# Adjacency masks cast to bf16 by GpSimd's transfers, and new hand-written orders, in a four-layer graph network

## What is computed

```
x = _layernorm(x + _L0_gnn_ref(x, adj, W0, a_src, a_dst))   # graph attention
x = _layernorm(x + _L1_gnn_ref(x, adj, W1, a1))             # graph attention
x = _layernorm(x + _L2_gnn_ref(x, adj, a0..a3, bias2))      # sigmoid attention
x = _layernorm(x + _L3_gnn_ref(x, adj, W3, bias3))          # relational conv
# layers 0 and 1: h = x @ W.T; e_ij = leaky_relu(h_i.a_src + h_j.a_dst, 0.2)
#   e = where(adj == 0, -inf, e); alpha = softmax(e, -1); return alpha @ h
# layer 2: e = leaky((x * a0) @ x.T, 0.2); alpha = sigmoid(where(adj == 1, e, -max))
#   return alpha @ x + bias2
# layer 3: h = (adj == 1) @ x; return h @ W3[0] + bias3
```

## Time and profile before

| | us |
|---|---|
| median of 3 runs | 260.65 (260.47 to 260.87) |
| the profiled execution | 259.62 |
| its span, first to last instruction | 257.1 |
| TensorE busy | 228.6 |
| VectorE busy | 226.5 |
| ScalarE busy | 206.5 |
| GpSimd busy | 173.6 |

### The profile page before, as it was taken

The page is one execution under the profiler, slowest core; times in us unless marked ns, Lnnn a source line. Parts: engine busy times, 40 slices in busy tenths (PEclk is TensorE's granted clock), DMA queues, the critical chain, the costliest instruction groups (busy, mean ns, idle before and its releaser), DMA issues.

```text
span 257.1 us, 5794 instructions
## 1 busy us (share of the span) xinstructions
PE 228.6 (89%) x1745; PEld 207.1 (81%) x1745; DVE 226.5 (88%) x794; ACT 206.5 (80%) x634; POOL 173.6 (67%) x248
## 2 busy tenths in 40 slices
PE   6869898998988999999999999999999988989670
PEld 6769788986977999879898888898979877887560
DVE  0498999989998999989999999999989998998851
ACT  3797999986867999878359965986895959989874
POOL 1003031759789988697357999867596876799892
PEclk9999999999999999999999999999999997999995
...
GB/s 243 402 387 213 209 92 259 166 18 0 1 85 0 126 124 134 71 41 46 41 125 82 3 1 0 42 4 51 34 0 3 3 42 42 42 41 0 43 41 129
DMA packets 12145, 21.77 MB, mean 85 GB/s; under 512 B 1104, under 2 KB 5968, under 8 KB 12112
## 3 DMA queue, kind: packets, MB, share of 16 engines
...
...
## 4 chain that ended last, share of the span: by engine, by line
PE 35%; DVE 23%; ACT 19%; POOL 13%; issue 6%; DMA 1%; POOLq 0%; DVEq 0%; ACTq 0%
PE banks L1176 13%; PE banks L1116 6%; POOL frstd L541 6%; DVE wgt_all L857 5%; DVE fstats L907 5%; PE banks L1143 4%; ACT odd_square L601 4%; POOL fxTa L565 4%; ACT xs_all L678 3%; PE banks L1173 3%; PE banks L1153 3%; DVE fres_all L899 3%; ACT wgt_all L651 3%; PE banks L1133 2%; ACT vals_all L636 2%
## 5 line engine op out<-in xcount | busy, mean ns | idle before, releaser
L541 POOL TENSOR_TENSOR frstd<-fvar,minus_half 128x4 f32<-128x4 f32 x64 | 65.1, 1020 | 36.5 <-ACT fvar L684 29.3
L1176 PE MATMUL banks<-vals_all,wgt_all 128*128 128x129 f32 x512 | 64.0, 279 | 3.4 <-issue 2.5
L1176 PEld LDWEIGHTS banks<-vals_all,wgt_all 128*128 128x128 f32 x512 | 60.6, 194 | 5.1 <-issue 3.1
L857 DVE SCALAR_TENSOR_TENSOR wgt_all<-banks,gain,mask_all 128x256 f32<-128x256 f32 x128 | 52.7, 471 | 1.9 <-PE banks L1133 1.9
L536 POOL TENSOR_TENSOR xb_all<-xs_all,bias_cen 128x256 f32<-128x256 f32 x64 | 45.5, 736 | 8.7 <-ACT xs_all L678 4.0
L907 DVE BATCH_NORM_STATS2 fstats<-fres_all 128x6 f32<-128x256 f32 x128 | 47.8, 417 | 0.5
L678 ACT ACTIVATE xs_all<-fres_all,frstd 128x128 f32<-128x128 f32 x124 | 39.5, 399 | 6.1 <-POOL frstd L541 6.0
L1143 PE MATMUL banks<-fxT,fxTa 128*128 128x256 f32 x128 | 31.3, 386 | 1.8 <-DVE wgt_all L865 0.6
L1176 PE MATMUL banks<-xs_all,wgt_all 128*128 128x128 f32 x256 | 31.4, 276 | 0.4 <-DVE wgt_all L865 0.4
L1176 PEld LDWEIGHTS banks<-xs_all,wgt_all 128*128 128x128 f32 x256 | 29.9, 192 | 0.9 <-DVE wgt_all L865 0.4
L565 POOL TENSOR_SCALAR fxTa<-fxT,w_pack 128x256 f32<-128x256 f32 x28 | 25.6, 930 | 6.4 <-ACT fxT L616 6.4
...
## 6 DMA issues: line engine op xcount, KB each, us to landing
...
```

The source lines that it names most:

```text
L541: nc.gpsimd.tensor_tensor(frstd[:, int(l), slot(n), :], fvar[:, int(l), slot(n), :], minus_half[:, :, :], ALU.pow).then_inc(fast_pool[k], 1)
L857: last = nc.vector.scalar_tensor_tensor(out=wgt(u)[:, c, :], in0=place(f"rows{l}", u), scalar=gain[:, u, c, 1:2], in1=maskT(u)[:, c, :], o ...
L1176: last = nc.tensor.matmul(place(f"out{l}", u)[:, b * width:(b + 1) * width], wgt(u)[:, c, b * P:(b + 1) * P], (vals if l in "01" else xs)( ...
```

## The change

The masks come from GpSimd's own transfers, which read int32 and write bf16 (`cast_mask`). The ring is as deep as there are teams, so all sixteen are issued first thing and never wait for a buffer; each has a semaphore of its own. The ring `adj_all` and SyncE's sixteen loads are gone, and so are ScalarE's mask steps; `seen` reads the mask. The masks are now 0 and 1, so `res2` multiplies by 0.5 instead, in the same instruction as its addition, and `w3_cen` isn't doubled. `xTa` of all teams and `norm1` of all teams are ScalarE's (before: 2 and 7 of the 16). VectorE has `norm2` of 2 teams instead of 1, `low` of 2 instead of 1, and `bias2` of one. All lists and the table of banks are written anew: before, teams 0 to 5 went through layers 0 and 1 together, and the last four ended in the order 13, 14, 15, 12; now the teams follow each other in a stagger, and after the start with teams 0 to 2 a new one comes in about as often as one leaves.

```diff
-X_IN, XT_IN, ADJ, MASK, XS, FXT, FXTA, VALS, WGT, SG, FRES, XB = 4, 3, 4, 10, 6, 7, 5, 6, 7, 2, 9, 5
-EDGE = 0.5
+X_IN, XT_IN, MASK, XS, FXT, FXTA, VALS, WGT, SG, FRES, XB = 4, 3, 16, 6, 7, 5, 6, 7, 2, 9, 5
 ORDER = {
     "sp": (
-        "xT:0 adj:0 adj:1 xT:1 xT:2 adj:2 adj:3 x:0 x:2 x:1 x:3 weights:0 xT:3 weights:2 weights:1 adj:4 xT:4 xT:5 "
+        "xT:0 x:0 xT:1 x:1 xT:2 weights:1 x:3 x:2 weights:0 weights:2 xT:3 xT:4 xT:5 x:4 x:5 x:6 xT:6 xT:7 x:7 xT:8 x:8 "
...
     "pool": (
-        "pow0:0 pow0:1 var0:2 pow0:2 var0:3 pow0:3 var0:4 pow0:4 pow1:0 norm1:0 bias2:0 pow0:5 xTa:0 pow1:1 bias2:1 "
+        "mask:0 mask:1 mask:3 mask:2 mask:4 mask:5 mask:10 mask:8 mask:6 mask:7 mask:9 mask:11 mask:12 mask:14 mask:15 "
+        "mask:13 var0:0 pow0:0 pow0:1 pow0:2 pow1:0 bias2:0 pow1:1 var0:3 pow0:3 pow1:2 bias2:1 bias2:2 var0:4 pow0:4 "
...
         @block.gpsimd
+            def cast_mask(l, n, k):
+                nc.gpsimd.dma_start(mask_all[:, pair(n, MASK), :, :], adj_turned[n]).then_inc(fast_mask_in[n], 16)
...
             def note_odd(l, n, k):
-                act.wait_ge(fast_adj_in[n % ADJ], loaded(n * H, ADJ))
+                act.wait_ge(fast_mask_in[n], 16)
...
-                nc.scalar.activation(odd_square[:, :, :, :], adj_all[:, pair(n, ADJ), :, :], ACT.Square, bias=minus_half[:, 0, 0:1],
+                nc.scalar.activation(odd_square[:, :, :, :], mask_all[:, pair(n, MASK), :, :], ACT.Square, bias=minus_half[:, 0, 0:1],
                                      accum_out=odd[:, n:n + 1]).then_inc(fast_act[k], 1)
-            def make_mask(l, n, k):
-                if n >= MASK:
-                    act.wait_ge(fast_pe[(n - MASK) % K], at("pe", "agg", final(n - MASK)))
-                act.wait_ge(fast_adj_in[n % ADJ], loaded(n * H, ADJ))
-                for u in graphs(n):
-                    nc.scalar.activation(maskT(u)[:, :, :], adj_in(u)[:, :, :], ACT.Copy, scale=EDGE).then_inc(fast_act[k], 1)
...
-                nc.vector.tensor_scalar(w3_cen[:, :], w3_cen[:, :], 1 / EDGE, None, ALU.mult).then_inc(w3_cen_set, 1)
...
             def weights(l, n, k):
                 dve.wait_ge(fast_pe[k], at("pe", f"rows{l}", final(n)))
                 if l == "0":
-                    masker = doer("mask", n)
-                    dve.wait_ge(signals[masker][k], at(masker, "mask", final(n)))
+                    dve.wait_ge(fast_mask_in[n], 16)
...
-                    nc.vector.tensor_tensor(fres_all[:, pair(n, FRES), :, :], gathered, xb_all[:, pair(n, XB), :, :], ALU.add).then_inc(fast_dve[k], 1)
+                    nc.vector.scalar_tensor_tensor(out=fres_all[:, pair(n, FRES), :, :], in0=gathered, scalar={"2": 0.5, "3": 1.0}[l],
+                                                   in1=xb_all[:, pair(n, XB), :, :], op0=ALU.mult, op1=ALU.add).then_inc(fast_dve[k], 1)
```

More of the change, by code:

```diff
@@ L418, in res_gnn_kernel @@
         biases_in = sem("biases_in")
[L419 removed]
+        fast_mask_in = [sem(f"fast_mask_in_{q}") for q in range(TEAMS)]
         fast_xT_in = [sem(f"fast_xT_in_{q}") for q in range(XT_IN)]
@@ L576, in scales @@
                 nc.gpsimd.tensor_tensor(fscale[:, slot(n), :], vals_all[:, pair(n, VALS), :, D], frstd[:, 0, slot(n), :], ALU.mult).then_inc(fast_pool[k], 1)
-            steps = {"bias": biases, "pow": powers, "low": low_part, "var": variances, "fscale": scales, "xTa": scale_xTa, "norm": normalize}
+            steps = {"mask": cast_mask, "bias": biases, "pow": powers, "low": low_part, "var": variances, "fscale": scales, "xTa": scale_xTa, "norm": normalize}
             for step, l, n in order("pool"):
@@ L939, in judge @@
                 nc.vector.tensor_reduce(bad[:, 8:9], bad[:, 3:7], AX.X, ALU.max).then_inc(bad_step, 1)
-            steps = {"mask": make_mask, "high": high_part, "umax": larger, "bias": biases, "low": low_part, "norm": normalize, "fscale": scales, "logits": logits, "peak": peak, "dmax": largest,
+            steps = {"high": high_part, "umax": larger, "bias": biases, "low": low_part, "norm": normalize, "fscale": scales, "logits": logits, "peak": peak, "dmax": largest,
                      "weight": weights, "rsum": row_sums, "rinv": inverses, "alpha": alpha, "res": residual,
```

31 lines of the change are left out of this document (8 added, 23 removed), and 192 rows, old and new, of tables (BANKS, ORDER).

## The result

The changed kernel takes 258.63 us, median of 20 runs (257.13 to 260.89); the kernel before took 260.60 in the same series (259.45 to 261.65). The ratio is 0.9922, 95% interval 0.9902 to 0.9943. The forecast was 259.1. So the time is right within half a microsecond, and the kernel is faster by 0.8%. Of the four terms behind the forecast none came out with its size, and they don't add up to the measured gain; the last part says how the number came out right all the same. A ratio here leaves out executions more than 1.5% above the fastest of the same kernel, while a median is of all, so a ratio needn't be the quotient of the two medians.

What follows compares the result with a forecast made beforehand. TensorE (228.6 us of 257.1) and VectorE (226.5) were taken to bind, with fill and tail. Terms +5.4 - 3.1 + 1.0 - 4.8 = -1.5 on 259.62 gave 258.1; with 1.03 to the median, 259.1; range 252.0 to 265.5.

Steps and rivals of the forecast that it cites:

- Term 1: Where the last layer 1 product ends: work moved ahead of that point puts it 5.4 us later, at 225.4.
- term 4: Gaps in the middle, 40 to 220 us: half of VectorE's 8.6 us close, small products gain 0.5; -4.8 us.
- Term 2: Tail behind the last layer 1 product: ScalarE sets the end, 34.0 us instead of 37.1; -3.1 us.
- Term 3: Fill at the start: first weight near 10 us, VectorE briefly idle before out1:0; +1.0 us, bounds 0 and +2.5.
- Only three teams in flight: In the fill, three teams instead of six leave VectorE with nothing to do from about 34.4 to 36.1 us.
- The masks by transfer: Loading at the start: casting transfers cost 0, issues of 1.0 us each on GpSimd hidden up to 1.45 us each.
- Rival C: Slow issuing on GpSimd delays the first power: 268 us at 2 us each, decides from 1.45; chance 0.12.
- sign of the prediction: When frstd, the first power's result on GpSimd, is first written: under 20 us for A, past 27 for Rival C.
- A: The forecast case, all four terms as priced: 259.1 us, within 256 to 262; chance 0.50.
- Rival E: Casting transfers at a quarter of the plain rate, 5.6 us a mask, block ScalarE: +16, 275 us; chance 0.07.
- No idle time that ends with a mask's landing: At the start, neither VectorE nor ScalarE would have idle time ended by a mask's landing.
- seven are in by 15 us: Mask loading at the start: at 1.5 us each, seven masks land by 15 us even beside 2 MB of other loads.

Runs made afterwards that it cites:

- the flag late: Changed kernel with one added wait, so VectorE writes the flag on which all engines branch to their end only after ScalarE's last norm3: 257.26 us, 0.9865 of the kernel before.

## Why the prediction was right, and where it was not

**Term 1, +5.4 for the place of the last layer 1 product: read from the wrong engine.** On TensorE most of it is there: behind that point it is busy 21.00 us instead of 25.65, 4.65 less, and ahead of it 209.5 instead of 202.9, some 2 us of that being products at half clock. But VectorE was busy 199.9 us ahead of the point before and 200.2 now. The prediction put VectorE's list beside TensorE's ("moves the same way") and added 2.8 us. Behind the point VectorE has only 1.8 us less (24.88, was 26.64), and its total fell by 1.4 instead. Without the shortening of the small products (term 4), 3.0 us, its work ahead of the point would have grown by 3.4. Of its three additions `bias2` came at the 0.8 us forecast, and the norms at 0.3 instead of 1.35, since the old team's norm had been among the lengthened instructions (mean 407 ns, now 272). `low` came at 2.2 instead of 0.8: three of its four instructions took 0.87 to 0.95 us instead of 0.42, while GpSimd was at a `low` or a `bias`.

```profile
L822 DVE TENSOR_TENSOR fscale<-vals_all,frstd 128x4 f32<-128x4 f32 x16 | 3.0, 191 | 0.2 <-ACT vals_all L611 0.2
L770 DVE TENSOR_TENSOR fxTa<-xs_all,fxTa 128x256 f16<-128x256 f32 x4 | 3.0, 784 | 0.3 <-ACT fxTa L643 0.3
L889 DVE SCALAR_TENSOR_TENSOR fvar<-fstats,fvar 128x4 f32<-128x4 f32 x16 | 2.9, 181 | 0.1
...
L790 DVE TENSOR_SCALAR xs_all<-fres_all,frstd 128x128 f32<-128x128 f32 x8 | 1.7, 272 | 0.0
```

**Term 2, the tail, -3.1: -1.6 measured.** The way to the last norm came out better than forecast: from the last layer 1 product to the last norm's end 30.0 us pass, where 31.25 were forecast and 34.3 stood before. Two errors hide in it. Behind `vals1:15` ScalarE was busy 26.6 us, not 30.1, since single steps overlap by some 0.1 us when they follow each other; and it waited 5.1 us, not 2.5, of which 2.5 are for the powers ahead of three of the last norms. What failed was the constant: the 2.75 us taken over from the earlier trace rows for the way from norm to end became 5.46. With the flag late the tail is 33.2 us (221.5 to 254.7), under the 34.0. Of the 2.7 us that the constant grew by, 0.7 came back outside the span (1.78 us, was 2.52), which the prediction held equal.

**Term 3, the fill, +1.0: mis-sized, 6.3 measured** (4.3 in the second profiled execution of the same kernel)**.** The prediction saw `seen:0` ahead of `gains0:0` and drew from it only that the first weight comes "near 10"; it did not ask when the mask lands for which `seen:0` waits. And it priced the `seen` steps as work, not by their place. Spreading them gave VectorE 27.8 of 40 us instead of 22.2 or 24.2, which leaves 0.7 us of loss against the 28.5 of before. So nearly the whole size is theirs, TensorE's clock included, which went with them in every profiled execution: `v0:2` stands behind `seen` steps in seven profiled executions of the new lists. In six of them the granted clock fell to 0.50 once between 12 and 30 us, and in the seventh a group of sixteen products took 3.65 us. In the four in which it stands ahead of them, neither happened. "Only three teams in flight" can't have been worth more than those 0.7.

**The masks by transfer, 0.** Rival C is excluded: an issue takes 0.54 to 0.76 us (rows at the end of this paragraph), against 1.0 taken and 1.45 where it would have decided, and `var0:0`, which stands ahead of `pow0:0`, waited for its statistics until 21.27. So neither sign of the prediction came: the first power ended at 22.6, not under 20 as for A nor past 27 as for C, and it was the fill that delayed it. Rival E is excluded too: the sixteen masks held the DMA engines for 8.9% of 257.8, 22.9 us or 1.43 each, where the old adjacency loads held them for 1.34 each (24.9% less 16.5% of the spans). The way of the masks alone, in the old orders, changed the time by 0.3% (0.9993 to 1.0061). Yet two statements fell. "No idle time that ends with a mask's landing": 6.6 us of ScalarE did. And "seven are in by 15 us": they shared the engines with the other loads, and half of them took over 16.2 us from issue to landing.

```profile
L516 POOL DMA_DIRECT2D mask_all<-adj_turned x16: 543/600/760, 1.8 to 9.8; - x16
...
  ACT odd_square L593: 6.6, 2
...
DMA to landing us min/median/max: 7.4/16.2/25.0
```

**Term 4, the middle, -4.8.** The gaps from 40 us to the last layer 1 product shrank by 4.4 us, where 4.3 was taken; but the half was a guess between none and all, and the runs don't say which wait went for which reason, so that this size was met is partly luck. The small products gave 3.0 instead of 0.5. The stretch around 214 with its clock at 0.50 is gone. The Trainium skill (SBUF — State Buffer, "Who interferes with whom") says that a VectorE instruction with two SBUF inputs contends with a GpSimd one that reads SBUF. For `low` and `bias` the traces agree; the powers read SBUF too, and none of the 28 products begun during one was longer than 200 ns, so there the measurement decides. The prediction scaled by GpSimd's total load, which is too coarse: in these traces a product is long where it meets one of GpSimd's additions. `fscale` alone gave 1.6 us, and `fvar`, which the prediction had not looked at, another 1.4. VectorE is busy 97.8% from 60 us on, as "over 96%" said.

**The sum.** The last product ended 2.3 us later. On VectorE's ledger that is 3.4 for the shift, -7.4 for the middle (4.4 of gaps, 3.0 of small products) and 6.3 for the fill; the forecast had 5.4, -4.8 and 1.0, together 1.6. So 2.0 and 2.6 us too many on one side stood against 5.3 too few on the other. With the tail the span grew by 0.7 us, where the forecast had it shrink by 1.5, and the profiled execution is 0.04 us shorter, not 1.5. The medians fell by 2.0 all the same, for the profiled execution of before lies 0.98 us below its median and that of the changed kernel 0.95 above. The second profiled execution of the changed kernel has a span of 254.8, 2.3 under that of before, but lies 2.2 below its median. Between these two the terms fit the medians as well as a profile can tell, about 2 us either way. The case came out as A, faster, by 0.8%; that 259.1 was met within 0.5 us is luck.
